# Graph network on one core: the first layer's gathers are released by the landing of the gather two ahead, no longer by TensorE's transposes

## Chip, core and metric

The kernel runs on one core of one Trainium2 chip. The metric is the device time of the whole program in microseconds (us), the median of several runs. TensorE is PE in the profile, VectorE is DVE, ScalarE is ACT, GpSimd is POOL, and SyncE, which only issues DMAs here, is SP.

## What is computed

Two message-passing layers on a graph of 12,500 nodes with 16 features and 412,500 edges sorted by destination. The change touches the first layer alone. Cut to what matters:

```python
h    = relu(edge_attr @ W1 + b1)                # 412500 x 256
w    = (h @ W2 + b2).reshape(-1, 16, 16)        # one 16 x 16 matrix per edge
msgs = einsum('ei,eio->eo', x[src], w)          # x[src]: the gather
aggr = segment_sum(msgs, dst)                   # per node
```

A normalisation of the nodes stands before it, a batch normalisation behind it, and the second layer repeats gather, product and sum with 8 edge features.

## The kernel before

`layer0` cuts the edges into G = 404 groups of 1,024: 8 tiles (T) of 128 edges. For each group, five engines run a loop of their own over the groups, written out by hand, and meet at semaphores (the dictionary `q`). `each_ring` runs a body four groups at a time, so that buffer numbers are constants: the first lap is written out, then a hardware loop, then the last lap.

- SP loads the edge features `ea` of a group (64 KB).
- POOL gathers: `gather(g, r, use)`, lines 795 to 805. For each of the 8 tiles one indirect DMA (L802) fetches 128 rows of 32 floats from `gather_rows` in DRAM into `xg[r]`, one of RING = 4 buffers; its landing raises the semaphore `xg_in[r][t]` by 16. Every fourth group (r = 3, from the second lap on) has only 7 gathers, because PE forms the last tile's rows from a table instead (L947). Ahead of the 8 gathers of a group stands one instruction that waits: for the indices (`idx_ready`, by ACT), for the buffer (`msg_ready` of the group four back, by DVE), and for `e_turned` of group g, which PE raises behind its 8 transposes of that group's edge features. Nothing that the gather reads or writes depends on those transposes. That instruction also adds one to `gathers_begun`, a counter on which nobody waits.
- ACT splits the edge features, copies the transposes out (L835), applies the relu (L841), makes the indices (L816) and splits the messages.
- PE, for each group g: the first product `hidden` (L905), the second product `edge_weights` (L919, two halves of 16 matmuls in float32), the transposes `turn(g + 2)` (L895, they raise `e_turned`), and `scatter(g - 1)` (L933, 16 small matmuls that sum messages into a window of nodes).
- DVE multiplies the edge matrices with the gathered rows in 4 units of 2 tiles (L1002), each of which waits for PE's `wmm` and for the two landings `xg_in`, reduces them (L1009), adds the bias (L1015, raises `msg_ready`), and makes the one-hot tables for the scatter (L1033).

PE transposes for group g + 2 while it works on group g, so a burst of 8 gathers starts about two groups ahead of its use. The second layer (`layer1`) has four scatters for each group on POOL (L1745), each with its own counting instruction ahead of it.

Of the kernel before, what the change touches and what calls it, by code (L numbers as in the profile page):

```python
# [51 lines left out]
def need(engine, sem, count):  # L52

    if isinstance(count, int) and count <= 0:
        return
    engine.wait_ge(sem, count)  # L56
# [15 lines left out]
def each_ring(engine, count, body, ring=4, laps=1):  # L72


    for c in range(laps * ring):
        body(c, c % ring, c // ring)
    assert count % ring == 0
    with engine.Fori(0, count // ring - laps - 1) as i:
        for u in range(ring):
            body(i * ring + (laps * ring + u), u, i + laps)  # L80
    for u in range(ring):
        c = count - ring + u
        body(c, u, c // ring)
# [626 lines left out]
def layer0(nc, S, k, sem, c, ea16, n_passes):  # L710
# [42 lines left out]
    q = {n: sem(n) for n in names}  # L753
    ea_in = [sem(f"ea_in{s}") for s in range(2)]
    xg_in = [[sem(f"xg_in{r}{t}") for t in range(T)] for r in range(RING)]
# [5 lines left out]
    def dense(r, lap):  # L761

        return r in DENSE and not (isinstance(lap, int) and lap == 0)
# [6 lines left out]
    with nc.Fori(0, n_passes) as _:  # L770
        with nc.Block() as block:

            @block.sync
            def _(sp):
                def load(g, r, lap):
                    s = r % 2
                    e0 = min(g * GE, S.E - GE) if isinstance(g, int) else sp.snap(g * GE)
                    need(sp, q["ea_used"], g - 1)
                    sp.dma_start(ea[s][:, :, :].rearrange("p t f -> p (t f)"),
                                 ea16[bass.ds(e0, GE), :].rearrange("(p t) f -> p (t f)", t=T)  # L780
                                 ).then_inc(ea_in[s], 16)
                    if dense(r, lap):
                        need(sp, q["col_free"], lap - 1)
                        sp.dma_start(col_b[:, :], k.col_rows[bass.ds(g, 1), :].broadcast_to([KP, P])
                                     ).then_inc(q["col_in"], 16)
                    if isinstance(g, int) and g == 1:
                        sp.dma_start(rows_in[:, :, :],
                                     k.rows[0:S.N, :].rearrange("(k p r) f -> p k (r f)", p=KP, r=KR)
                                     ).then_inc(q["node_in"], 16)
                each_ring(sp, G, load, RING, 2)  # L790
                clear_tables(sp, S, k, q["zeroed"])

            @block.gpsimd
            def _(pool):
                def gather(g, r, use):
                    pool.wait_ge(q["idx_ready"], g + 1)
                    need(pool, q["msg_ready"], g - RING + 1)
                    if not (isinstance(g, int) and g < 2):
                        pool.wait_ge(q["e_turned"], g + 1)
                    pool.sem_inc(q["gathers_begun"], 1)  # L800
                    for t in range(T - 1 if dense(r, use) else T):
                        pool.indirect_dma_start(  # L802
                            xg[r][:, t, :], None, k.rows,
                            bass.IndirectOffsetOnAxis(ap=idx[r][:, t:t + 1], axis=0)
                        ).then_inc(xg_in[r][t], 16)
                each_ring(pool, G, gather, RING)

                pool.wait_ge(q["msg_ready"], G)
                pool.dma_reset()
# [1206 lines left out]
```

## Time and profile before

| what | value |
|---|---|
| runs shown | 8242.69 us median of 3 (8239.94 to 8244.3) |
| profiled execution, span from the first to the last instruction | 8221.3 us |
| PE, PEld, DVE, ACT, POOL busy | 89%, 78%, 81%, 54%, 69% |
| mean granted TensorE clock | 0.947 of full speed |
| L802, the gathers | 3132, busy 3041.9 us, mean 971 ns; POOL idle before them 1882.4 us |
| L919, the second product | 12928 matmuls, busy 3240.2 us |
| DMA | mean 42 GB/s over the span, about 17 GB/s in the first layer |

For the profiled execution only its span is given; it is 21.4 us below the median of the runs, and what lies around the span is taken as that. Busy means that an engine was executing; an engine can be idle because it waits for another or because its instruction has not reached it. In a timeline row the bracket holds the idle time before the row and what ended it. "issue" there means that no wait ended that the profile shows, and "remote" that the releaser was not an instruction of this list.

### The profile page before, as it was taken

To read this page: it belongs to the slowest core of one execution; us is meant where nothing else is said; L and a number is where in the kernel's file an instruction comes from. 1 tells how busy PE (TensorE), PEld (TensorE's weight loads), DVE (VectorE), ACT (ScalarE), POOL (GpSimd) and SP (SyncE) were. 2 spreads that over 40 slices of the span, in tenths; PEclk is the share of its full clock that TensorE was granted. 3 is DMA by queue.
4 is the path that set the end of the run, shared out by engine and by line. 5 is a ranking of instruction groups with operands and counts; after the bars stand their busy time and mean duration, and the time that the engine had idled before them with its cause. 6 is when DMAs were issued, how large, how long until landed. Compare 5 with 4: busy or idle time off the path is not lost. (4 is left out here: it accounts for less than half of the span.)

```text
span 8221.3 us, 191064 instructions
## 1 busy us (share of the span) xinstructions
PE 7349.2 (89%) x52997; PEld 6446.6 (78%) x52997; DVE 6691.0 (81%) x17449; ACT 4457.4 (54%) x8279; POOL 5696.0 (69%) x4866
## 2 busy tenths in 40 slices
PE   7888888888888888888888886999999999999998
PEld 5667676666676666666676765999999999999996
DVE  6777777777777777777777777999999999999997
ACT  3333333333333333333333335888888878778884
POOL 6666666666666666666666664888888888888886
PEclk8999999999999999999999998999999999999999
DMA  2000000000000000000000014444444455554443
GB/s 60 18 17 17 17 17 17 17 17 17 17 17 17 17 18 17 17 17 18 17 17 17 17 23 101 73 75 74 74 75 74 74 73 74 72 74 75 73 75 64
DMA packets 713464, 341.73 MB, mean 42 GB/s; under 512 B 422115, under 2 KB 656599, under 8 KB 713427
## 3 DMA queue, kind: packets, MB, share of 16 engines
q1 hardware_dynamic: 379313, 272.94, 13.1%
q0 software_dynamic: 332928, 64.86, 12.9%
q10 hardware_dynamic: 1186, 3.51, 0.1%
q8 instruction: 15, 0.25, 0.0%
q14 instruction: 22, 0.18, 0.0%
HBM read 307.85 MB, written 32.96 MB: 41 GB/s over the span
## 5 line engine op out<-in xcount | busy, mean ns | idle before, releaser
L802 POOL DMA_INDIRECT xg<-gather_rows,idx x3132 | 3041.9, 971 | 1882.4 <-issue 1848.5
L919 PE MATMUL ps_w<-W2s,hT 128*128 128x256 f32 x12928 | 3240.2, 408 | 37.1 <-issue 36.6
L919 PEld LDWEIGHTS ps_w<-W2s,hT 128*128 128x128 f32 x12928 | 2678.5, 207 | 581.6 <-issue 97.0
L1745 POOL DMA_INDIRECT sums<-total,row x1616 | 2551.0, 1579 | 529.1 <-issue 474.4
L1708 PE MATMUL ps_wide<-hot_col,placed 128*128 128x392 f32 x12928 | 2434.7, 345 | 4.8 <-DVE placed L1544 2.1
L1708 PEld LDWEIGHTS ps_wide<-hot_col,placed 128*128 128x128 f32 x12928 | 2313.6, 196 | 12.2 <-issue 6.9
L841 ACT ACTIVATE hT<-ps_h,b1c 128x512 f32<-128x512 f32 x1616 | 1022.8, 680 | 2302.1 <-PE ps_h L905 2090.8
L1002 DVE TENSOR_TENSOR prod<-ps_w,xg 128x512 f32<-128x512 f32 x1616 | 1098.1, 690 | 969.7 <-remote 599.7
L1544 DVE SCALAR_TENSOR_TENSOR placed<-ps_r,src_r,halves 128x512 fp32r<-128x512 f32 x1616 | 1097.5, 741 | 0.1
L1643 ACT ACTIVATE square<-iota_col,minus_col 128x784 bf16<-128x784 int16 x1212 | 1061.3, 938 | 66.6 <-issue 58.0
L1009 DVE TENSOR_REDUCE msg<-prod 128x32 f32<-128x512 f32 x1616 | 1058.9, 676 | 0.0
L1649 ACT ACTIVATE hot_col<-square,ones 128x2352 fp32r<-128x2352 bf16 x404 | 910.4, 2253 | 0.0
L933 PE MATMUL ps_a<-parts,hot 128*128 128x48 bf16 x6464 | 347.5, 184 | 549.8 <-issue 534.0
L1033 DVE TENSOR_SCALAR hot<-iota,rel_t 128x256 bf16<-128x256 bf16 x3232 | 729.1, 303 | 116.0 <-DVE ea_res L982 73.0
L933 PEld LDWEIGHTS ps_a<-parts,hot 128*128 128x128 bf16 x6464 | 249.8, 96 | 580.4 <-issue 566.4
L905 PE MATMUL ps_h<-eT,W1p 96*128 96x512 bf16 x1616 | 526.5, 401 | 147.5 <-issue 137.8
L1682 PE MATMUL ps_q<-q_win,hotT 128*128 128x128 bf16 x9696 | 609.6, 219 | 18.9 <-DVE hotT L1483 18.9
L1501 DVE TENSOR_TENSOR prod<-ps_q,e 128x512 f32<-128x512 f32 x808 | 552.3, 684 | 42.6 <-issue 40.4
L1682 PEld LDWEIGHTS ps_q<-q_win,hotT 128*128 128x128 bf16 x9696 | 548.1, 98 | 20.0 <-DVE hotT L1483 20.0
L1510 DVE TENSOR_REDUCE pre<-prod 128x64 f32<-128x512 f32 x808 | 548.3, 679 | 0.1
L851 ACT ACTIVATE parts<-msg_res 128x128 bf16<-128x128 f32 x404 | 124.9, 309 | 552.9 <-DVE msg_res L1021 322.9
L835 ACT ACTIVATE eT<-ps_e 96x1024 bf16<-96x1024 bf16 x404 | 409.1, 1013 | 1.9 <-PE ps_e L895 1.9
(229 smaller groups left out, 5425.0 us busy)
## 6 DMA issues: line engine op xcount, KB each, us to landing
dst_row<-dst_rows SPq DMA_DIRECT2D x404, 256.0 KB
src_row<-src_rows SPq DMA_DIRECT2D x404, 128.0 KB
xg<-gather_rows,idx POOLq DMA_INDIRECT x3132
q_win<-q_rows SPq DMA_DIRECT2D x404, 96.0 KB
ea<-in_edge_attr SPq DMA_DIRECT2D x404, 64.0 KB
sums<-total,row POOLq DMA_INDIRECT x1616
e<-in_edge_attr SPq DMA_DIRECT2D x404, 32.0 KB
q_rows<-Q SPq DMA_DIRECT2D x12, 768.0 KB, 5.4
```

The lines of the kernel that those rows point to most:

```text
L802: pool.indirect_dma_start(xg[r][:, t, :], None, k.rows, bass.IndirectOffsetOnAxis(ap=idx[r][:, t:t + 1], axis=0)).then_inc(xg_in[r][t], 16)
L841: a.activation(hT[s][:, j, :], ps_h[j][:, :], ACT.Relu, bias=k.b1[:, j:j + 1]).then_inc(q["relued"], 1)
L919: last = pe.matmul(to, hT[half][:, j, col:col + P], k.W2[:, j, :], start=(j == 0), stop=(j == 1 and not with_b2))
L1002: v.tensor_tensor(prod[u % 2][:, :, :, :], ps_w[u][:, :, :, :], xg[r][:, 2 * u:2 * u + 2, 0:D].unsqueeze(2).broadcast_to([P, 2, D, D]), AL ...
L1009: v.tensor_reduce(msg[s][:, 2 * u:2 * u + 2, :], prod[u % 2][:, :, :, :], X, ALU.add).then_inc(q["reduced0"], 1)
L1033: last = v.tensor_scalar(hot[s][:, t, :], k.iota[:, :], k.rel[:, bass.ds(g, 1), t:t + 1].rearrange("p g t -> p (g t)"), None, ALU.is_equal)
L1544: last = v.scalar_tensor_tensor(placed[s][:, w, :, :, :].rearrange("p r f a -> p r (f a)"), ps_r[:, :, :], src_r[:, bass.ds(g, 1), w], hal ...
L1643: last = a.activation(square[:, n, :], iota_col[:, :], ACT.Square, bias=minus_col[:, bass.ds(g, 1), WIDE - ACT_TILES + n])
L1649: a.activation(hot_col[s][:, WIDE - ACT_TILES:, :, :].rearrange("p w a b -> p (w a b)"), square[:, :, :].rearrange("p w b -> p (w b)"), AC ...
L1682: last = pe.matmul(ps_q[u][:, w, :, :].rearrange("p h j -> p (h j)"), hotT[s][:, t * P:(t + 1) * P], q_win[s][:, part * P:(part + 1) * P], ...
L1708: last = pe.matmul(ps_wide[:, 2 * r + a, 0:S.LC], placed[s][:, w, r * HR:(r + 1) * HR, :, part].rearrange("p r f -> p (r f)"), hot_col[s][ ...
L1745: pool.indirect_dma_start(k.sums[t], bass.IndirectOffsetOnAxis(ap=row[r][:, t:t + 1], axis=0), total[r][:, t, :], None, compute_op=ALU.add ...
```

## The change

Two edits in `gather`. The wait for `e_turned` goes. From the third tile of a group on (t >= 2), each gather has in front of it an instruction that waits until gather t - 2 of the same group has landed (its semaphore at 16 for each use of the buffer) and adds one to `gathers_begun`. So the first two gathers of a group wait for indices and buffer alone.

```diff
                 def gather(g, r, use):
                     pool.wait_ge(q["idx_ready"], g + 1)
                     need(pool, q["msg_ready"], g - RING + 1)
-                    if not (isinstance(g, int) and g < 2):
-                        pool.wait_ge(q["e_turned"], g + 1)
                     pool.sem_inc(q["gathers_begun"], 1)
                     for t in range(T - 1 if dense(r, use) else T):
+                        if t >= 2:
+                            pool.wait_ge(xg_in[r][t - 2], 16 * (use + 1))
+                            pool.sem_inc(q["gathers_begun"], 1)
                         pool.indirect_dma_start(
                             xg[r][:, t, :], None, k.rows,
                             bass.IndirectOffsetOnAxis(ap=idx[r][:, t:t + 1], axis=0)
```

No instruction of PE, DVE, ACT or SP moves. On POOL, in the hardware loop of the first layer, the first two groups of a lap stood like this before (a row with x7 is seven gathers in a row; the waits are those in front of the row):

```order
L56 REGISTER_ALU [waits idx_ready]
L802 DMA xg<-gather_rows,idx 128x32 [waits msg_ready,e_turned]
L802 DMA xg<-gather_rows,idx 128x32 x7
L796 REGISTER_ALU
L56 REGISTER_ALU [waits idx_ready]
L802 DMA xg<-gather_rows,idx 128x32 [waits msg_ready,e_turned]
L802 DMA xg<-gather_rows,idx 128x32 x7
```

and stand now like this (the second group of the lap; xg_in1t is the landing of tile t in buffer 1):

```order
L56 REGISTER_ALU [waits idx_ready]
L803 DMA xg<-gather_rows,idx 128x32 [waits msg_ready]
L803 DMA xg<-gather_rows,idx 128x32
L803 DMA xg<-gather_rows,idx 128x32 [waits xg_in10]
L803 DMA xg<-gather_rows,idx 128x32 [waits xg_in11]
L803 DMA xg<-gather_rows,idx 128x32 [waits xg_in12]
L803 DMA xg<-gather_rows,idx 128x32 [waits xg_in13]
L803 DMA xg<-gather_rows,idx 128x32 [waits xg_in14]
L803 DMA xg<-gather_rows,idx 128x32 [waits xg_in15]
```

The wait for PE's transposes is gone from the head of the burst, and six waits on landings stand inside it (five in a group of 7 gathers). The gathers themselves keep their order and their number.

## Rows read from the trace of the kernel before

**Rows 1.** Busy time by stretch; 62 to 4960 us is the first layer
```profile
core 0: us, PE busy (x) PEld busy (x) DVE busy (x) ACT busy (x) POOL busy (x), PEclk, DMA share, GB/s
...
500.00:4500.00 4000.00, 3406.92 (x20511) 2782.20 (x20510) 2907.68 (x8081) 1572.46 (x3299) 2479.31 (x2557) 0.92 0.10 17
...
4960.00:8221.00 3261.00, 3152.24 (x27836) 3026.12 (x27834) 3093.25 (x7509) 2507.20 (x4189) 2627.17 (x1696) 0.98 0.50 75
```
**Rows 2.** Groups by line, 500 to 4500 us (busy us, mean ns, idle before)
```profile
L919 PE MATMUL ps_w<-W2s,hT 128*128 128x256 f32 x10558 | 2641.5, 407 | 28.3 <-issue 27.8 <-DVE prod L1002 0.3
L802 POOL DMA_INDIRECT xg<-gather_rows,idx x2557 | 2480.0, 970 | 1523.2 <-issue 1522.6 <-ACT idx L816 0.6
...
L1002 DVE TENSOR_TENSOR prod<-ps_w,xg 128x512 f32<-128x512 f32 x1319 | 895.9, 690 | 801.5 <-remote 509.6 <-issue 165.1 <-PE ps_w L919 43.6
...
L933 PE MATMUL ps_a<-parts,hot 128*128 128x48 bf16 x5264 | 286.1, 184 | 453.8 <-issue 450.0
```
**Rows 3.** Timeline of POOL, three bursts (start us, duration us)
```profile
2510.22 0.95 POOL L802 DMA_INDIRECT xg<-gather_rows,idx  x1 [0.30 <-issue]
2513.62 0.94 POOL L802 DMA_INDIRECT xg<-gather_rows,idx  x1 [2.45 <-issue]
2514.87 0.94 POOL L802 DMA_INDIRECT xg<-gather_rows,idx  x1 [0.30 <-issue]
...
2522.72 0.94 POOL L802 DMA_INDIRECT xg<-gather_rows,idx  x1 [0.30 <-issue]
2526.03 0.94 POOL L802 DMA_INDIRECT xg<-gather_rows,idx  x1 [2.37 <-issue]
...
2537.02 0.94 POOL L802 DMA_INDIRECT xg<-gather_rows,idx  x1 [2.57 <-issue]
```
**Rows 4.** Timeline of PE, 2500 to 2526 us
```profile
2501.09 5.30 PE L919 MATMUL ps_w<-W2s,hT 128*128 128x256 f32 x16
2506.23 0.60 PE L905 MATMUL ps_h<-eT,W1p 96*128 96x512 bf16 x2
2506.67 3.62 PE L919 MATMUL ps_w<-W2s,hT 128*128 128x256 f32 x16
2510.12 0.61 PE L895 MATMUL ps_e<-identb,ea_parts 128*96 128x128 bf16 x8
2510.57 0.44 PE L933 MATMUL ps_a<-parts,hot 128*128 128x48 bf16 x11
2511.18 0.19 PE L933 MATMUL ps_a<-parts,hot 128*128 128x48 bf16 x1 [0.18 <-issue]
2512.60 0.27 PE L933 MATMUL ps_a<-parts,hot 128*128 128x48 bf16 x4 [1.23 <-issue]
```
**Rows 5.** Timeline of DVE, the multiply that waits in each burst
```profile
2512.68 0.69 DVE L1002 TENSOR_TENSOR prod<-ps_w,xg 128x512 f32<-128x512 f32 x1 [1.51 <-remote]
...
2525.20 0.69 DVE L1002 TENSOR_TENSOR prod<-ps_w,xg 128x512 f32<-128x512 f32 x1 [1.65 <-remote]
```
**Rows 6.** POOL's waiting instruction L800, window 2504 to 2505 us
```profile
L800 POOLq EVENT_SEMAPHORE  x1: 8643/8643/8643, 2504.2 to 2504.2; - x1
```
**Rows 7.** DMA traffic, 2510 to 2514 us, 40 slices of 0.1 us
```profile
DMA  0000005610000000004530000000000000000000
GB/s 0 0 0 0 0 0 82 72 10 0 0 0 0 0 0 0 0 0 61 62 41 0 0 0 0 0 0 0 0 0 0 0 0 0 0 0 0 0 0 0
```
**Rows 8.** Timeline, the layer's first burst of 16 gathers
```profile
68.26 1.09 PE L895 MATMUL ps_e<-identb,ea_parts 128*96 128x128 bf16 x8 [0.48 <-DVE ea_parts L989]
68.60 0.95 POOL L802 DMA_INDIRECT xg<-gather_rows,idx  x1 [0.30 <-issue]
69.03 0.26 PEld L905 LDWEIGHTS ps_h<-eT,W1p 96*128 96x128 bf16 x2
69.14 1.06 PE L905 MATMUL ps_h<-eT,W1p 96*128 96x512 bf16 x2
69.38 1.02 ACT L835 ACTIVATE eT<-ps_e 96x1024 bf16<-96x1024 bf16 x1 [0.35 <-PE ps_e L895]
```
**Rows 9.** Groups by line, second layer, 5000 to 8000 us
```profile
L1745 POOL DMA_INDIRECT sums<-total,row x1549 | 2446.2, 1579 | 507.4 <-issue 454.1 <-ACT row L1635 37.1 <-DMA sums<-total,row 16.2
L1708 PE MATMUL ps_wide<-hot_col,placed 128*128 128x392 f32 x12416 | 2336.5, 345 | 4.8 <-DVE placed L1544 2.1 <-issue 0.8
```

## Prediction

> **What bounds the kernel now.** I read the busy time by stretch first. The second layer, from 4960 us on, is not touched; PE and DVE are busy there for 3152 and 3093 of 3261 us. The first layer is looser: in 4000 us PE is busy for 3407, DVE for 2908, POOL for 2479 [rows 1]. The group count of that stretch is that of the second product's matmuls over the 32 of a group, 10558 / 32 = 329.9 [rows 2]. So one group takes 4000 / 329.9 = 12.12 us, and in it PE is busy for 10.33 us, DVE for 8.81 us and POOL for 7.52 us. No engine is full, so a wait that comes back in each group sets the pace.
>
> The groups by line show where. POOL idles 1522.6 us before its gathers, DVE 509.6 us before the multiply, released by something "remote", and PE 450 us before the scatter matmuls with nothing named [rows 2]. The timelines say how these hang together. POOL starts a gather every 1.25 us (0.94 us of work and 0.30 us between two); a burst of eight begins at 2513.62 us, its last gather at 2522.72 us, and the next burst only at 2526.03 us [rows 3]. Between them are 2.4 us of idle POOL. PE ends its transposes at about 2510.7 us (start 2510.12, eight of them) and then hardly moves: one scatter matmul at 2511.18 us, the next at 2512.60 us [rows 4]. At 2512.68 us DVE's multiply is let go, after 1.51 us of idleness; the product it waits for ended on PE 2.4 us before, at 2506.67 + 3.62 = 2510.29 us. The next such release is at 2525.20 us [rows 5]. Both lie 2.46 and 2.48 us behind the start of the burst's last gather, at 2510.22 and 2522.72 us [rows 3, 5]. POOL's waiting instruction is busy from 2504.2 us for 8.64 us, so to 2512.9 us, although the transposes it waits for were done at 2510.7 us [rows 6].
>
> I read it so: while POOL stands in its long wait with gathers still queued behind each other, signals of the other engines come late, and they come through once the last gather has landed. POOL waits for a signal that its own gathers hold back. Two rows speak for this. In the layer's first burst PE ends its transposes at 68.26 + 1.09 = 69.35 us, in the middle of sixteen gathers at the same spacing, and ACT starts on them at 69.38 us, at once; POOL had no wait for PE there [rows 8]. In the second layer POOL issues a DMA of 1.58 us after another, at 4 to 5 times the traffic, and PE loses 4.8 us in 3000 [rows 1, 9]. Why the signals are held, no row tells.
>
> **The change, part by part.** *The wait for the transposes goes.* With it goes the tail between the last gather's start and the next burst, 2526.03 - 2522.72 = 3.31 us, of which 1.25 us would be there in any case. What holds POOL next is the buffer (the message of the group four back), and that is far: POOL is two groups ahead now and may be three ahead.
>
> *A wait on a landing is added before the gathers 2 to 7 of a group.* Its price is the landing time L of a gather from its start, and the time D from the end of a wait to the start of the gather behind it. D is 2513.62 - 2512.9 = 0.73 us [rows 3, 6]. L is not shown and is bounded from both sides: the gather of 2510.22 us has its data packets until 2512.1 us, so L is at least 1.9 us [rows 7]; everything that waited was released 2.47 us after the last start, so L is at most that [rows 3, 5]. I take 2.2 us, midway, since the rise of the semaphore follows the last data packet and the release of the others follows that rise. Then gather t starts L + D = 2.93 us after gather t - 2, where it now starts 2.50 us after it. The two chains, of the even and of the odd tiles, run beside each other, 1.25 us apart. A group of eight lasts 3 x 2.93 for the tiles 2, 4 and 6, and 2 x 1.25 to the next group's first gather, which has no landing to wait for: 11.29 us. A group of seven lasts 10.04 us. The mean over a lap of 3 and 1 is 10.98 us. The gathers last 0.97 us on the mean and not 0.94 [rows 2, 3]; for 7.75 of them that adds 0.2 us: **11.18 us a group**.
>
> The Trainium skill (DMA: Bandwidth & Descriptors, "Anatomy of one DMA — SWDGE (gpsimd) path") puts such a DMA at about 2.0 us and bytes / 436,000, which for the 16 KB of a gather is 2.04 us. By it the step would be 2.77 us, the group 10.70 us, and the whole 574 us shorter than now, about 7668 us. The packets end 1.9 us after the start [rows 7], so the trace does not speak against it, but no row shows the landing itself.
>
> *The counting instructions and register steps* (six more on POOL in a group of eight) are issued while the engine works on the gather before; the gap of 0.30 us stays the same in the second layer, where each DMA has such an instruction. If that cover failed, it would cost at most D again, which is already in the sum. DVE, queued for the landings, gets them later by up to 11.3 - 10 = 1.3 us within a burst, but the burst starts two to three groups ahead of use.
>
> *Who is the bound then.* PE needs at most its 10.33 us. In that are matmuls at the lower clock: the granted clock is 0.92 on the mean in this stretch [rows 1], and the sixteen matmuls right after PE's halt took 5.30 us where the next ones took 3.62 us [rows 4]. DVE needs 8.81 us. Both are under 11.18 us: POOL becomes the bound.
>
> *Sum.* (12.12 - 11.18) x 404 groups = 380 us. The profiled execution's span of 8221.3 us becomes 7841 us; with the 21.4 us by which the median lies above the span, **7862 us**. Ends: with L = 1.9 us the group is 10.28 us, PE's 10.33 us takes over, -723 us, 7520 us. With L = 2.47 us it is 11.99 us, -53 us, 8190 us.
>
> **Rivals.**
> 1. *The signals stay late, and the spread-out burst makes it worse* (the other side). POOL now stands in a wait of about half to one us before nearly every gather, with another gather in flight, and the burst is never quiet. If any waiting of POOL beside gathers holds back signals, as the long one does, PE and DVE get free only behind the last landing of a burst, and the bursts are longer. For: PE's halt, from 2511.2 to 2512.6 us, falls beside the last gather of a burst, while POOL stands in its wait [rows 3, 4, 6]. Against: rows 8, and the short waits end often. Price: last gather at 3 x 2.93 + 1.25 + 0.2 = 10.24 us, and the present tail of 3.31 us: 13.55 us, 12.3 us for seven, 13.24 us on the mean; +1.12 x 404 = +452 us, 8695 us. It decides as soon as more than 0.94 us a group of the halt is left on top of POOL's 11.18 us.
> 2. *The halts are PE's own.* PE's scatter stops for a reason that has nothing to do with POOL's wait, POOL's idle time was harmless, and PE's 10.33 us and its 1.8 us of idleness stay: 12.12 us a group, no change, 8243 us. Against it: DVE's release comes 2.46 and 2.48 us behind the last gather's start in two bursts in a row [rows 3, 5], which fits POOL's clock and not PE's.
> 3. *Half of it.* The long hold goes, a short delay for each signal stays, and PE with its dependences needs about 11.65 us: -190 us, 8053 us. This lies inside the forecast's own bounds.
> 4. *The waits never bite.* That would need L + D under 2.5 us, and 1.9 + 0.73 is 2.63 us. Then the group would fall to PE's 10.33 us, 7520 us. I give it 2 in 100.
>
> **How the numbers follow.** The forecast with POOL as the bound has 0.58, half of it (3) 0.05, no bite (4) 0.02, no change (2) 0.05, slower (1) 0.30. This measurement tells about 0.2%, 16 us, from no change. So faster 0.65, same 0.05, slower 0.30. The forecast's own range is 7520 to 8190 us. The range for 8 in 10 leaves out its lowest tail, under 7600 us (0.04), and the half of rival 1 that lies above 8560 us (0.15): 7600 to 8560 us.
>
> **What would show it.** Right: POOL's timeline alternates between 1.25 and about 1.7 us from start to start, with no gap of 2.4 us at the end of a burst; the group takes about 11.2 us; DVE's idle time before the multiply names the landings or shrinks; PE's scatter matmuls run without single steps; the granted clock of the stretch rises or stays. The landing time can then be read as the step of two gathers less 0.73 us. Wrong: PE's single steps beside gathers are as many as before, or spread over the whole group (rival 1 if the group is above 12.12 us, rival 2 if POOL is seen waiting on the buffer at an unchanged pace). The size is wrong if the step of two gathers is not near 2.93 us.

## The result, and the profile after

| kernel | median | runs | profiled execution, span |
|---|---|---|---|
| before | 8243.49 us | 8239.94 to 8244.47 | 8221.3 us |
| changed | 8299.38 us | 8278.49 to 8306.21 (4 runs) | 8294.4 us, clock 0.949 |

The ratio is 1.0064, with a 95% interval of 1.0052 to 1.0075: the change made the kernel slower by 0.6%, where the prediction had it faster by 4.6%. The time lies inside the range, 7600 to 8560 us, and on the side that had 0.30. Line numbers behind `gather` grow by one: L803 is the gather, L842 the relu, L920 the second product.

Busy time of the changed kernel in the stretch of [rows 1]:

```profile
core 0: us, PE busy (x) PEld busy (x) DVE busy (x) ACT busy (x) POOL busy (x), PEclk, DMA share, GB/s
500.00:4500.00 4000.00, 3356.24 (x20304) 2671.17 (x20303) 2874.96 (x7991) 1544.30 (x3263) 2416.86 (x2528) 0.93 0.10 17
```

The groups by line in that stretch (busy us, mean ns of one, idle before and what ended it), to be read against [rows 2]:

```profile
L920 PE MATMUL ps_w<-W2s,hT 128*128 128x256 f32 x10438 | 2619.7, 406 | 44.4 <-issue 29.1 <-DVE prod L1003 11.3
L803 POOL DMA_INDIRECT xg<-gather_rows,idx x2528 | 2417.4, 956 | 1583.4 <-issue 1014.7 <-DMA xg<-gather_rows,idx 484.2 <-ACT idx L817 83.6
...
L1003 DVE TENSOR_TENSOR prod<-ps_w,xg 128x512 f32<-128x512 f32 x1304 | 873.3, 689 | 236.7 <-issue 53.2 <-remote 43.3 <-DVE hot_c L1044 22.4
...
L842 ACT ACTIVATE hT<-ps_h,b1c 128x512 f32<-128x512 f32 x1306 | 827.9, 680 | 1883.7 <-remote 1384.6 <-PE ps_h L906 393.6 <-issue 101.7
...
L906 PE MATMUL ps_h<-eT,W1p 96*128 96x512 bf16 x1304 | 423.9, 407 | 540.1 <-ACT eT L836 394.7 <-issue 142.6 <-ACT hT L842 0.8
...
L934 PE MATMUL ps_a<-parts,hot 128*128 128x48 bf16 x5216 | 198.6, 183 | 42.0 <-issue 37.7 <-DVE win_sum L1094 1.5
...
L983 DVE TENSOR_TENSOR ea_res<-ea,ea_parts 128x128 f32<-128x128 f32 x326 | 95.0, 291 | 709.9 <-ACT ea_parts L823 432.7 <-issue 276.9
```

A group now takes 4000 / (10438 / 32) = 12.26 us, 0.14 us more than before; over 404 groups that is 57 us, the whole difference of the medians (56 us). The old waits went, as forecast: PE's idle time before the scatter fell from 453.8 to 42.0 us, DVE's before the multiply from 801.5 to 236.7 us, and the "remote" share of the latter from 509.6 to 43.3 us. Others took their place. The first product on PE (L906) waits 540.1 us where it waited 108.6 us before, and DVE waits 709.9 us where it waited 108.0 us to work on the edge features that ACT splits (L983), so its gain before the multiply is used up elsewhere. And the relu on ACT, which before was released by PE, is now let go by "remote" for 1384.6 us. The kernel before, same stretch:

```profile
L841 ACT ACTIVATE hT<-ps_h,b1c 128x512 f32<-128x512 f32 x1319 | 835.2, 680 | 1886.1 <-PE ps_h L905 1748.9 <-remote 79.7 <-issue 41.8
...
L905 PE MATMUL ps_h<-eT,W1p 96*128 96x512 bf16 x1318 | 429.7, 401 | 108.6 <-issue 105.3 <-ACT hT L841 1.6 <-ACT eT L835 1.5
...
L982 DVE TENSOR_TENSOR ea_res<-ea,ea_parts 128x128 f32<-128x128 f32 x330 | 95.4, 289 | 108.0 <-issue 79.8 <-ACT ea_parts L822 27.1
```

POOL, PE and ACT of the changed kernel in time (start us, duration us), to be read against [rows 3, 4]:

```profile
2513.57 0.94 POOL L803 DMA_INDIRECT xg<-gather_rows,idx  x1 [0.30 <-issue]
2515.49 0.94 POOL L803 DMA_INDIRECT xg<-gather_rows,idx  x1 [0.98 <-issue]
2516.74 0.94 POOL L803 DMA_INDIRECT xg<-gather_rows,idx  x1 [0.30 <-issue]
2518.64 0.94 POOL L803 DMA_INDIRECT xg<-gather_rows,idx  x1 [0.96 <-DMA xg<-gather_rows,idx]
```
```profile
2514.53 0.56 PE L934 MATMUL ps_a<-parts,hot 128*128 128x48 bf16 x16
2514.94 0.59 PE L906 MATMUL ps_h<-eT,W1p 96*128 96x512 bf16 x2
2515.37 3.62 PE L920 MATMUL ps_w<-W2s,hT 128*128 128x256 f32 x16
2522.32 1.03 PE L906 MATMUL ps_h<-eT,W1p 96*128 96x512 bf16 x2 [3.33 <-issue]
```
```profile
2520.01 1.26 ACT L842 ACTIVATE hT<-ps_h,b1c 128x512 f32<-128x512 f32 x2 [7.40 <-remote]
```

POOL's pauses of 2.4 us between bursts are gone; it alternates between steps of 1.25 us and about 1.9 us, 3.15 us for two (2515.49 to 2518.64). PE's scatter runs its sixteen matmuls without a stop. But the product `ps_h` that the relu at 2520.01 us needs ended on PE at 2514.94 + 0.59 = 2515.53 us. Measured from there, the signal came 4.5 us late (the profile models the ends of matmuls, so this is a lag behind a modelled end), ACT could not copy the transposes out behind it, and PE's next first product started after 3.33 us of idleness. The late signals did not go away. They moved, from one that the scatter and the multiply wait for to one that the relu waits for.

All of them are signals of PE. In the first layer of every run below with late signals, "remote" stands only in front of work that waits for PE: the relu, the multiply and, in the kernel before, POOL's gathers. The trace's records of semaphores say the same. In the kernel before, from 500 to 3500 us, 246 of the 247 recorded signals of the transposes come more than 0.5 us behind the last transpose, at most 6.1 us; of ACT's and DVE's recorded signals none lags its instruction.

### The profile page after: what moved, and what is told of

Same layout as the page of the kernel before. It is cut to its first block and busy times, and to the rows that moved or that the text cites. A ratio compares the mean times of both kernels' runs of the same rounds, so it can differ in the third digit from the quotient of the medians.

```text
span 8294.4 us, 193483 instructions
## 1 busy us (share of the span) xinstructions
PE 7333.8 (88%) x52997; PEld 6345.0 (76%) x52997; DVE 6680.6 (81%) x17449; ACT 4443.1 (54%) x8279; POOL 5653.6 (68%) x4866
## 5 line engine op out<-in xcount | busy, mean ns | idle before, releaser
L803 POOL DMA_INDIRECT xg<-gather_rows,idx x3132 | 3001.6, 958 | 1996.5 <-issue 1259.3
L920 PE MATMUL ps_w<-W2s,hT 128*128 128x256 f32 x12928 | 3244.2, 406 | 63.0 <-issue 33.9
L920 PEld LDWEIGHTS ps_w<-W2s,hT 128*128 128x128 f32 x12928 | 2632.5, 205 | 627.7 <-issue 126.7
L842 ACT ACTIVATE hT<-ps_h,b1c 128x512 f32<-128x512 f32 x1616 | 1024.7, 680 | 2288.5 <-remote 1662.2
L906 PE MATMUL ps_h<-eT,W1p 96*128 96x512 bf16 x1616 | 526.8, 407 | 656.3 <-ACT eT L836 480.1
L983 DVE TENSOR_TENSOR ea_res<-ea,ea_parts 128x128 f32<-128x128 f32 x404 | 117.7, 291 | 858.3 <-ACT ea_parts L823 512.2
L906 PEld LDWEIGHTS ps_h<-eT,W1p 96*128 96x128 bf16 x1616 | 137.0, 97 | 811.5 <-issue 769.9
```

Source lines behind the costliest of these rows:

```text
L803: pool.indirect_dma_start(xg[r][:, t, :], None, k.rows, bass.IndirectOffsetOnAxis(ap=idx[r][:, t:t + 1], axis=0)).then_inc(xg_in[r][t], 16)
L842: a.activation(hT[s][:, j, :], ps_h[j][:, :], ACT.Relu, bias=k.b1[:, j:j + 1]).then_inc(q["relued"], 1)
L920: last = pe.matmul(to, hT[half][:, j, col:col + P], k.W2[:, j, :], start=(j == 0), stop=(j == 1 and not with_b2))
```

## The experiments

Each session sent one to four kernels to one chip, and the kernel before ran beside them there. The sessions fall into two sorts: the kernel before takes 7298 us in some and 8173 us or more in others, and stays within 0.2% inside each.

| session, number of the chip | before in it | this kernel | ratio (95%) |
|---|---|---|---|
| the result | 8243.49 | changed 8299.38 | 1.0064 (1.0052 to 1.0075) |
| e1 to e4, 7 | 7298.18 | below | |
| e5, e6, 5 | 7298.32 | changed 8126.28 | 1.1136 (1.1118 to 1.1155) |
| e7 to e9, 0 | 8175.45 | below | |
| e10 to e12, 4 | 7298.71 | below | |
| e13, e14, 2 | 8174.14 | below | |
| e15, e16, 6 | 8173.44 | changed 8150.99 | 0.9973 (0.9961 to 0.9985) |
| e17, 6 | 7298.69 | below | |
| e18, 1 | 7298.13 | below | |

I call the two sorts sessions with holds and sessions without; a hold is such a late signal of PE. The session of the result has holds too. The expectations written on the way call them chips with and without holds; that was premature, since two sessions that name chip 6 fell on either side.

### e1 to e4: the parts of the change one by one, and no gathers

**e1** takes the wait for the transposes away and adds nothing:

```diff
-                    if not (isinstance(g, int) and g < 2):
-                        pool.wait_ge(q["e_turned"], g + 1)
```

> The wait for PE's transposes is gone, no wait on landings is added. Theory A (a gather in flight holds back the other engines' signals, whatever POOL itself waits for): a burst now starts as soon as its buffer is free and is no longer placed so that its tail falls on PE's scatter; the holds stay as many and fall on the relu handshake. 8300 to 8600 us, PE's idle time before L905 as in the changed kernel or more. Theory B (POOL's waiting instruction holds them back): POOL waits only for the buffer, 3 groups ahead; 7700 to 8100 us.

Measured: 7300.17 us, ratio 1.0001 (0.9992 to 1.0011).

**e2** keeps that wait and adds the waits on landings:

```diff
                     for t in range(T - 1 if dense(r, use) else T):
+                        if t >= 2:
+                            pool.wait_ge(xg_in[r][t - 2], 16 * (use + 1))
+                            pool.sem_inc(q["gathers_begun"], 1)
```

> The landing waits are added, the wait for PE's transposes stays. Theory A: the burst of eight lasts 3 x 3.13 + 1.25 = 10.6 us to the start of its last gather instead of 9.1, and the pause behind it stays: a group of 12.1 + 1.5 = 13.6 us, 8243 + 600 = about 8850 us. Theory B: the same or a little less, 8600 to 8850 us. A third reading (the holds come only from gathers 1.25 us apart): the holds vanish, a group is about 12.1 us, 8243 us.

Measured: 8129.4 us, ratio 1.1138 (1.1119 to 1.1156).

**e3** adds the counting alone:

```diff
+                        if t >= 2:
+                            pool.sem_inc(q["gathers_begun"], 1)
```

> Only the counting instruction is put in front of each gather from the third on, without a wait. It costs nothing on a queue that runs ahead of its engine: theories A and B both say 8243 us within 16 us. If pacing of POOL's queue by such an instruction is what frees the signals (as in the second layer), it is faster, below 8200 us.

Measured: 7299.32 us, ratio 1.0001 (0.9992 to 1.0011).

**e4** gathers for the first four groups only (DVE's waits on the landings go with the gathers, in a part of the edit that is not shown):

```diff
+                    if not (isinstance(g, int) and g < RING):
+                        return
                     for t in range(T - 1 if dense(r, use) else T):
```

> Left out: all gathers of the first layer from the fifth group on (the rows of the first four groups are used again), with DVE's waits on them. Theories A and B: the holds go with them and PE is the bound at 10.3 us a group or less, 8243 - 1.8 x 404 = 7520 us or less. Rival (PE's halts are its own): no change, 8243 us.

Measured: 7235.3 us, ratio 0.9912 (0.9895 to 0.9929).

None of the delays of the first profile appear on this chip, and the four tell what the parts cost by themselves. Counting: nothing. The wait for the transposes: nothing. All gathers together: 63 us. The waits on landings: 831 us. e1 did not test my theory, as there was nothing held to set free; the times expected for e1 to e3 had assumed holds and were missed, and e4's, 7520 us or less, fits a layer without holds in any case.

### e5 and e6: both kernels again, to see this other regime

The kernels of the change and of before, without an edit.

> The changed kernel as it is, on the chip of this job, against the kernel before in the same job. Where the kernel before takes 7298 us (no holds, PE is the bound at 9.8 us a group), the landing waits make POOL the bound at 11.3 to 11.8 us a group, as with both waits: 7900 to 8130 us, 8 to 11% slower. Where the kernel before takes 8243 us (signals held), 8299 us again.

> The kernel before, for its profile on this chip. Without holds: PE's scatter without single steps, no idle time of DVE before the multiply released by something remote, granted clock 1.00 in the first layer, POOL's pauses at the end of a burst under 1 us. With holds: as in the profile of before.

Measured: changed 8126.28 us against 7298.32 us, ratio 1.1136 (1.1118 to 1.1155); e6, one run, 7304.75 us. The kernel before without holds, 500 to 3500 us (its first layer ends earlier):

```profile
core 0: us, PE busy (x) PEld busy (x) DVE busy (x) ACT busy (x) POOL busy (x), PEclk, DMA share, GB/s
500.00:3500.00 3000.00, 2883.93 (x18937) 2314.94 (x18938) 2653.91 (x7455) 1453.99 (x3041) 2258.30 (x2359) 1.00 0.12 21
```
```profile
L802 POOL DMA_INDIRECT xg<-gather_rows,idx x2359 | 2258.5, 957 | 741.8 <-issue 732.0 <-ACT idx L816 7.3 <-DVE msg L1015 2.4
L919 PE MATMUL ps_w<-W2s,hT 128*128 128x256 f32 x9728 | 2222.8, 381 | 31.7 <-DVE prod L1002 31.7
...
L1002 DVE TENSOR_TENSOR prod<-ps_w,xg 128x512 f32<-128x512 f32 x1217 | 812.8, 689 | 176.6 <-issue 45.7 <-DVE hot_c L1043 33.2
```

PE is busy for 96% of the time at full clock, a group takes 3000 / (9728 / 32) = 9.87 us, nothing is released by "remote", and POOL issues gather after gather at 1.25 us. And the changed kernel there (e5), 500 to 4500 us:

```profile
L920 PE MATMUL ps_w<-W2s,hT 128*128 128x256 f32 x10795 | 2578.8, 392 | 64.9 <-DVE prod L1003 64.1
L803 POOL DMA_INDIRECT xg<-gather_rows,idx x2612 | 2479.3, 949 | 1522.7 <-DMA xg<-gather_rows,idx 933.5 <-issue 578.9 <-ACT idx L817 10.3
...
L1003 DVE TENSOR_TENSOR prod<-ps_w,xg 128x512 f32<-128x512 f32 x1348 | 900.7, 688 | 869.9 <-DMA xg<-gather_rows,idx 683.9 <-PE ps_w L920 64.0 <-issue 48.1
L842 ACT ACTIVATE hT<-ps_h,b1c 128x512 f32<-128x512 f32 x1348 | 848.5, 680 | 694.9 <-PE ps_h L906 691.2 <-issue 3.3
```

A group takes 4000 / (10795 / 32) = 11.86 us. POOL waits for landings and DVE for POOL's gathers: POOL is the bound, cleanly, as the prediction had it, only at a higher price. (11.86 - 9.87) x 404 = 804 us, against 828 us measured. The page of this kernel also gives the landing time that the prediction had to bound (the last number, us from issue to landing; the page of the changed kernel in the first result has the same line, and so has e8's, in a session with holds):

```profile
xg<-gather_rows,idx POOLq DMA_INDIRECT x3132, 2.4
```

With L = 2.40 us and D = 0.73 us [rows 3, 6] the step of two gathers is 3.13 us; POOL's timeline in e5 has 3.20 us and 3.09 us for two such steps:

```profile
2506.43 0.94 POOL L803 DMA_INDIRECT xg<-gather_rows,idx  x1 [0.95 <-DMA xg<-gather_rows,idx]
...
2509.63 0.94 POOL L803 DMA_INDIRECT xg<-gather_rows,idx  x1 [1.00 <-DMA xg<-gather_rows,idx]
...
2512.72 0.95 POOL L803 DMA_INDIRECT xg<-gather_rows,idx  x1 [0.90 <-DMA xg<-gather_rows,idx]
```

### e7 to e9: what holds the signals

All three met a session with holds. **e7** is the changed kernel with `t >= 3` and `t - 3` in place of 2, so the waits allow three gathers in flight.

```diff
-                        if t >= 2:
-                            pool.wait_ge(xg_in[r][t - 2], 16 * (use + 1))
+                        if t >= 3:
+                            pool.wait_ge(xg_in[r][t - 3], 16 * (use + 1))
```

> No wait for the transposes; from the fourth gather on each waits for the landing of the gather three ahead. Theory C (on a chip without holds the whole cost of the change is POOL's chain: landing 2.40 us + 0.73 us from the wait's end to the next start = 3.13 us a step): a step of three gathers lasts 3.75 us anyway, the wait ends at 2.40 us, 0.62 us ahead of need; no cost, 7298 us within 16 us. Theory D (waiting instructions inside the burst cost by themselves, whatever they wait for): between 7298 and 8126 us, in the middle. If the chip of this job holds signals (kernel before at 8243 us), theory A says about 8250 us or more.

Measured: 9092.6 us, ratio 1.112 (1.1102 to 1.1139).

**e8** is the changed kernel with `t >= 1` and `t - 1`: a gather waits for the one right ahead of it. Only the first gather of a group still starts 1.25 us behind the last one of the group before.

```diff
-                        if t >= 2:
-                            pool.wait_ge(xg_in[r][t - 2], 16 * (use + 1))
+                        if t >= 1:
+                            pool.wait_ge(xg_in[r][t - 1], 16 * (use + 1))
```

> Each gather from the second on waits for the landing of the one in front of it. Theory C: 3.13 us from gather to gather, 7 x 3.13 + 1.25 = 23.2 us for a group of eight, 20.0 us for seven, 22.4 us on the mean; 7298 + (22.4 - 9.8) x 404 = about 12390 us, and 3.13 us can be read from POOL's timeline. Any other step contradicts the sum of the two.

Measured: 12498.75 us (one run).

**e9** is the kernel before with one more load of 400 KB in each group, issued by SP:

```diff
+                    if not (isinstance(g, int) and g < 2 * RING):
+                        sp.wait_ge(q["node_ready"], 1)
+                        need(sp, q["hog"], 16 * (g - 2 * RING))
+                        sp.dma_start(rows_in[:, 0, :], k.rows[0:KP * KR, :].rearrange("(p r) f -> p (r f)", r=KR)
+                                     ).then_inc(q["hog"], 16)
```

> The kernel before with one more load of 400 KB for each group of the first layer on SP's queue (data that nobody reads), some 40 GB/s more than the 21 GB/s there are. Theory E (the holds of the first profile are a matter of DMA traffic of any kind beside the gathers): PE's single steps and late releases appear, 7600 to 8300 us. Rival (the traffic has nothing to do with them): 7298 us within 60 us.

Measured: 8185.7 us, ratio 1.0012 (1.0002 to 1.0023), at 51 GB/s in place of 17.

The relu's row of e8, 500 to 4500 us:

```profile
L842 ACT ACTIVATE hT<-ps_h,b1c 128x512 f32<-128x512 f32 x704 | 442.6, 679 | 367.0 <-PE ps_h L906 366.8
```

And two gathers of e8 where two groups meet:

```profile
2502.25 0.94 POOL L803 DMA_INDIRECT xg<-gather_rows,idx  x1 [2.12 <-DMA xg<-gather_rows,idx]
2503.49 0.94 POOL L803 DMA_INDIRECT xg<-gather_rows,idx  x1 [0.30 <-issue]
```

e8 is the telling one. It is slow, because every gather but the first of a group waits out a landing (4000 / (5649 / 32) = 22.66 us a group, where 22.4 us were expected), but "remote" has gone from the relu altogether, although POOL stands in more and longer waits than anywhere else: it is idle for 2708 of 4000 us. So POOL's waiting does not hold signals; a run of gathers that overlap does. With one in flight, and two for about 1.15 us of each group (2502.25 + 2.40 - 2503.49), nothing is held. e7 allows three, but with 1.25 us from start to start and a landing after 2.40 us the third starts when the first is in, so two is the most; there the relu waits 2101.9 us for "remote", and 1384.6 us in the changed kernel (another session), whose two overlap for less of the time. Three times the bytes moved by SP's loads change next to nothing (e9), so it is not traffic of that kind; no expectation for e9 had covered a session with holds.

Overlap alone is not enough either. In the kernel before, a burst began at 2501.16 us, and in the middle of it the relu starts 0.42 us behind the start of its product:

```profile
2506.23 0.60 PE L905 MATMUL ps_h<-eT,W1p 96*128 96x512 bf16 x2
...
2506.65 1.26 ACT L841 ACTIVATE hT<-ps_h,b1c 128x512 f32<-128x512 f32 x2 [0.58 <-issue]
```

In the bursts that began at 2501.16 and 2513.62 us, and in e13's of 2499.63 us below, the last signal of PE that passes at once is recorded 5.7, 7.2 and 5.8 us behind the burst's first gather; the later ones are held until about the last landing. What decides it, no run shows.

### e10 to e12: three parts in one session

e10 is e1's kernel, e11 is e2's. **e12** moves the copies to SP and makes them plain: fixed rows of the same table in the same size, not the edges' own, and POOL has nothing to do in the layer:

```diff
+                    need(sp, q["msg_ready"], g - RING + 1)
+                    for t in range(T - 1 if dense(r, lap) else T):
+                        sp.dma_start(xg[r][:, t, :], k.rows[P * t:P * (t + 1), :]
+                                     ).then_inc(xg_in[r][t], 16)
...
-                        pool.indirect_dma_start(
-                            xg[r][:, t, :], None, k.rows,
```

> Again the wait for the transposes alone taken away. On a chip where the kernel before takes about 8200 us (signals held, as on the chips of the first result and of the run with lag three): theory F (overlapping gathers hold signals; the old wait keeps the end of each burst, where all is released, next to PE's scatter, and so protects the relu handshake): about 9090 us, as with lag three, whose waits hardly bite. If instead the waits of lag three cost there, it is nearer to 8200 us. On a chip where the kernel before takes 7298 us: 7300 us again.

> Again the landing waits with the wait for the transposes kept. On a chip that holds signals, theory F: the last gather of a burst starts at 3 x 3.13 + 1.25 = 10.6 us instead of 9.1 us and the pause of 3.3 us stays, if signals are held to the end of the burst: 13.6 us a group, about 8800 us. If two gathers that overlap only in part let signals through, POOL's chain of 11.8 us a group is the bound: 8130 to 8300 us. On a chip without holds 8129 us again.

> Changed: the rows of the first layer are fetched by plain copies of the same size (128 rows of 128 bytes, fixed rows) that SP issues, 8 or 7 a group, in place of POOL's indirect gathers. On a chip that holds signals: if POOL's own DMAs (their descriptors written by POOL) are the cause, the holds go and the time is near 7300 us; if any overlapping DMAs of 128 short rows do it, it stays near 8200 us or above. On a chip without holds: 7240 to 7300 us.

Measured: e10 7298.85 us, ratio 0.9999 (0.999 to 1.0009); e11 8128.52 us, 1.1138 (1.112 to 1.1157); e12 7293.69 us, 0.9994 (0.9984 to 1.0004). The session had no holds. It repeats e1 and e2 and settles nothing about the holds.

### e13 and e14: the two parts in a session with holds

The kernels of e1 and e2 again.

> The wait for the transposes alone taken away, hoped for on a chip that holds signals (kernel before at about 8200 us). Theory F (the old wait keeps the release at the end of each burst next to PE's scatter): about 9090 us, as with lag three. Rival (the waits of lag three made its cost): nearer to 8200 us. On a chip without holds 7300 us, which tells nothing new.

> The landing waits with the wait for the transposes kept, hoped for on a chip that holds signals. Theory F with signals held to the end of a burst: 13.6 us a group, about 8800 us. If signals come through at the seams between two gathers that overlap only in part: POOL's chain of 11.8 us is the bound, 8130 to 8300 us.

Measured: e13 9123.77 us, ratio 1.1158 (1.1125 to 1.119); e14 8161.43 us, ratio 0.9985 (0.9973 to 0.9996). This is the experiment that e1 should have been, and it contradicts the prediction head on: taking away the wait that I held to be the culprit costs 950 us (the expectation for it, made after e7, was near: 9090 us). The rows of e13, 500 to 4500 us (two lines fewer in `gather`, so L800 is the gather, L839 the relu, L917 the second product):

```profile
500.00:4500.00 4000.00, 3170.39 (x17346) 2373.44 (x17345) 2476.73 (x6826) 1300.53 (x2784) 2044.34 (x2158) 0.88 0.08 15
```
```profile
L917 PE MATMUL ps_w<-W2s,hT 128*128 128x256 f32 x8906 | 2548.5, 428 | 544.7 <-issue 530.8 <-DVE prod L1000 5.7
L800 POOL DMA_INDIRECT xg<-gather_rows,idx x2158 | 2044.6, 947 | 1956.0 <-ACT idx L814 1347.9 <-issue 608.1
...
L839 ACT ACTIVATE hT<-ps_h,b1c 128x512 f32<-128x512 f32 x1114 | 700.6, 679 | 2255.3 <-remote 2235.9 <-PE ps_h L903 17.8 <-issue 1.3
```

And its timelines, POOL, then ACT, then PE:

```profile
2499.63 0.94 POOL L800 DMA_INDIRECT xg<-gather_rows,idx  x1 [5.01 <-ACT idx L814]
...
2508.36 0.94 POOL L800 DMA_INDIRECT xg<-gather_rows,idx  x1 [0.31 <-issue]
2514.26 0.94 POOL L800 DMA_INDIRECT xg<-gather_rows,idx  x1 [4.96 <-ACT idx L814]
```
```profile
2511.14 1.26 ACT L839 ACTIVATE hT<-ps_h,b1c 128x512 f32<-128x512 f32 x2 [8.34 <-remote]
2513.20 0.21 ACT L814 ACTIVATE idx<-src_t 128x8 int32 x1
```
```profile
2509.55 0.47 PE L917 MATMUL ps_w<-W2s,hT 128*128 128x256 f32 x1 [0.34 <-issue]
2510.26 0.38 PE L917 MATMUL ps_w<-W2s,hT 128*128 128x256 f32 x1 [0.24 <-issue]
```

Here the loop can be read off. A burst runs from 2499.63 us, its last gather starts at 2508.36 us. The relu comes 2.78 us behind that start, so 0.38 us behind a landing of 2.40 us: its signal is held to the end of the burst. ACT makes the indices for the next burst only behind that relu, at 2513.20 us, and the burst starts at 2514.26 us. The sum is 8.73 + 2.78 + 2.06 + 1.06 = 14.63 us; the mean group is 4000 / (8906 / 32) = 14.37 us (every fourth burst has one gather less). So a burst holds the very signal on which the next one depends, and the two take turns. PE itself stutters in the same stretch: its second product runs in single matmuls with pauses between (L917 idles 530.8 us by "issue", where e6 has 31.7 us, all of it a wait for DVE), though within such a run of eight matmuls no wait stands in the program. So it is not only that others hear of PE late; "held signal" names what the waiting engine sees. e7 does the same (14.31 us a group): a wait for the gather three back hardly bites, since three steps of 1.25 us are 3.75 us and L + D is 3.13 us.

### e15 and e16: plain copies and the change, in a session with holds

e15 is e12's kernel, with the same fixed rows; e16 is the changed one.

> Plain copies of fixed rows, issued by SP, in place of POOL's gathers (same sizes, 8 or 7 a group), hoped for on a chip that holds signals. If POOL's own DMAs (descriptors written by POOL) are the cause of the holds: about 7300 us, as on the chip without holds. If any overlapping DMAs of 128 short rows hold signals: 8200 us or more. On a chip without holds 7294 us again.

> The changed kernel once more, hoped for on a chip that holds signals, in the same job as the kernel before. There the landing waits alone gave 8161 us and the missing wait for the transposes is now free to put the holds on the relu handshake: above 8174 us by about the 0.6% of the first result, 8200 to 8240 us. On a chip without holds 8126 us again.

Measured: e15 7303.43 us, ratio 0.8937 (0.8911 to 0.8963); e16 8150.99 us, ratio 0.9973 (0.9961 to 0.9985). With the copies on SP the layer runs at its pace without holds, in a session where the kernel before takes 8173 us. Its rows, 500 to 3500 us, and then SP's copies of one group in its timeline:

```profile
500.00:3500.00 3000.00, 2886.88 (x18979) 2319.21 (x18978) 2653.08 (x7466) 1457.45 (x3048) 0.00 (x0) 1.00 0.11 21
```
```profile
L833 ACT ACTIVATE hT<-ps_h,b1c 128x512 f32<-128x512 f32 x1220 | 767.1, 679 | 514.7 <-PE ps_h L897 514.4
```
```profile
2505.21 3.64 SPq L792 DMA_DIRECT2D xg<-gather_rows  x8
```

Each transfer has the size it had, a group has as many, they wait for no transposes and for no landings, they overlap more densely (eight issued within 3.64 us, each landing 1.7 us later), and nothing is "remote". The 870 us that such a session adds to the kernel before belong to POOL's overlapping gathers.

And e16, 500 to 4500 us:

```profile
L920 PE MATMUL ps_w<-W2s,hT 128*128 128x256 f32 x10753 | 2578.8, 394 | 19.9 <-DVE prod L1003 11.8 <-issue 4.9
...
L842 ACT ACTIVATE hT<-ps_h,b1c 128x512 f32<-128x512 f32 x1344 | 853.1, 681 | 1495.3 <-remote 967.2 <-PE ps_h L906 446.2 <-issue 79.8
```

The same kernel as in the first result, at 11.90 us a group: there are holds still, 967.2 us before the relu, but they add only 0.04 us to POOL's own 11.86 us. The expectation of 8200 to 8240 us, which took the first result's 0.6% for a property of such sessions, was missed.

### e17 and e18: plain copies issued by POOL

What e15 leaves open is whether it takes POOL as the issuer, the indirect addressing or the scattered rows. These keep POOL and its waits, without the one for the transposes, and copy fixed rows:

```diff
-                        pool.indirect_dma_start(
-                            xg[r][:, t, :], None, k.rows,
-                            bass.IndirectOffsetOnAxis(ap=idx[r][:, t:t + 1], axis=0)
-                        ).then_inc(xg_in[r][t], 16)
+                        pool.dma_start(xg[r][:, t, :], k.rows[P * t:P * (t + 1), :]
+                                       ).then_inc(xg_in[r][t], 16)
```

> The e_turned wait removed, and the gathers replaced by plain copies of the same size (128 rows of 128 bytes, fixed rows, not the edges' own), still issued by POOL with the same waits for indices and buffer. On a chip where the kernel before takes about 7298 us every theory expects about 7300 us. On a chip where it takes about 8174 us: if any overlapping DMAs issued by POOL hold back signals, holds as in the kernel without the e_turned wait (9124 us there), at least over 7600 us, with ACT's relu released by 'remote'; if it takes the indirect addressing, 7300 us as with the copies on SP.

> The kernel of e17 again, which had a chip without holds (before 7298.69 us there). If this chip shows holds (before about 8174 us): plain overlapping copies by POOL hold back signals if it comes above 7600 us; it takes the indirect addressing if it comes at about 7300 us.

Measured: 7290.35 us, ratio 0.9989 (0.9979 to 0.9998), and 7293.48 us, ratio 0.9994 (0.9985 to 1.0004). Both sessions had no holds, so neither decides it.

## Why the prediction was wrong

In sessions with holds the two edits give these times:

| | no waits on landings | waits on landings |
|---|---|---|
| wait for transposes | 8174 (before; 8243 in the result's session) | 8161 (e14) |
| no wait for transposes | 9124 (e13) | 8151 (e16; 8299 in the result's session) |

And without holds: 7298 (before) and 8129 (e2) in the upper row, 7300 (e1) and 8126 (e5) in the lower. The waits on landings put the kernel on POOL's chain, 8126 to 8161 us in e2, e5, e14 and e16, each in a session of its own; that happens to be about as long as the kernel before is with its holds, and the change trades one for the other.

**The step that failed first: "POOL waits for a signal that its own gathers hold back", so that without this wait the holds go.** The first half stands, for PE's signals: they come through behind a burst's last landing [rows 5, 6], and e8, e13 and e15 show it in three ways. The prediction spoke of the signals of the other engines; those of ACT and DVE are never seen late. The second half was wrong. The holds need gathers in flight, not a waiting POOL (e8: POOL waits most, nothing is held), and taking POOL's wait away alone makes them dearer (e13, +950 us). By its rows, the wait for the transposes did useful work by its place: the late part of each burst fell beside scatter and multiply, which cost 2.25 us a group (12.12 - 9.87), while the relu's signal passed early in the burst. Without it, the late part of a burst meets the relu's handshake, from which the first product and the next burst's indices hang, and that costs 4.50 us a group (14.37 - 9.87, each from another session). That it is the place which does it is my reading of the timelines; no run moved the burst by itself. It also shows that the prediction named the wrong next wait: not the buffer of the group four back, but the indices (1347.9 us before the gathers of e13). In the result the holds moved to the relu just so, 1384.6 us before it. I had taken the signal at 69.38 us [rows 8], which came at once beside sixteen gathers, for proof that a POOL without such a wait holds nothing. Two things were wrong with it. Signals pass early in steady bursts too. And POOL did stand in a wait for PE there: its waiting instruction for the third group began at 69.1 us and lasted 18.04 us, in the kernel before:

```profile
L800 POOLq EVENT_SEMAPHORE  x1: 18044/18044/18044, 69.1 to 69.1; - x1
```

In that same burst PE's next recorded signal, of the second product that ended at 74.31 us, stands at 77.65 us in the trace's semaphore records, 3.3 us late. Nor did [rows 9] say what I took from it: the second layer's DMAs also overlap, starting some 1.9 us apart (1.58 and 0.30 us) and landing after 3.0 us (e6's page), and PE loses little there with holds or without; why they do so little, no run shows.

**The term that was mis-sized: L.** I took 2.2 us between the ends 1.9 and 2.47 us; it is 2.40 us. By the prediction's own formula a group of eight then takes 3 x 3.13 + 2 x 1.25 = 11.89 us, one of seven 10.64 us, the mean 11.58 us, with 0.2 us for the longer gathers 11.78 us. Measured without holds: 11.86 us. The form of the sum was right, and its upper end (11.99 us, 8190 us) was the place to be. A release 2.47 us behind the last start [rows 5] was the nearer row: it is a signal that has passed, where the end of the data packets at 1.9 us [rows 7] is only traffic. The Trainium skill (DMA: Bandwidth & Descriptors, "Anatomy of one DMA — SWDGE (gpsimd) path") gives 2.04 us by its figures. The trace has 2.4 us for the indirect gather, so the measurement decides, and the estimate by the page, 7668 us, was further off than mine; POOL's plain copies of the same size landed after 2.0 us (e17), as the page has it.

**The parts together.** The first result lies 8299 - 8126 = 173 us above the same kernel without holds. That rest, 12.26 - 11.86 = 0.40 us a group, or 162 us, is what the remaining holds add on top of POOL's chain. In e16 they add 0.04 us. Why the first result had more of them than e16, the runs don't tell.

**D, 0.73 us, was right.** L + D = 3.13 us, and the steps measured are 3.09 to 3.20 us, which with L = 2.40 us leaves 0.69 to 0.80 us for D.

**The counting at nothing was right** (e3, ratio 1.0001).

**PE's need of 10.33 us was too high.** It holds matmuls at the lower clock behind each halt. Undisturbed, the clock is 1.00 in the stretch and the group 9.87 us (e6). It played no part, as POOL was slower in any case.

**The marks.** No pause of 2.4 us, no single steps in the scatter, DVE's idle time before the multiply less, the clock of the stretch no lower (0.93 after 0.92): these all came, and the time still rose. They were marks of the old holds alone and would not have caught a hold at another handshake. The mark of size did catch it: a step of two of 3.15 us where 2.93 us was said.

**The rivals.** Rival 1, "the signals stay late", is the one that came about, but not as priced. It set the tail of 3.31 us on top of a whole burst, 13.24 us a group and 8695 us; measured are 12.26 us. I read it so, untested: with waits on landings there is a stretch in each step of two, from a landing to the next gather's start, in which one gather alone is in flight, and signals get through near it (the gather of 2516.74 us lands at 2519.14 us, the next starts at 2519.89 us, the relu at 2520.01 us). Its point of decision, more than 0.94 us a group on top of 11.18 us, was passed with 1.08 us, of which some 0.68 us is POOL's own chain (11.86 - 11.18) and 0.40 us holds. Rival 2, PE's own halts, is excluded by e15, where they are gone in a session with holds. Rival 3, half of the gain at 8053 us, lay 246 us too low. Rival 4 is excluded by each POOL timeline.

**What stays open.** What makes a session one with holds: not the kernel, as the same file ran in both, and not simply the chip's number. Whether POOL's plain copies hold signals too (e17, e18). How POOL's gathers can hold PE's signals and not those of ACT and DVE, and whether it is the signal that is late or PE's completion of the matmul, whose end the profile only models. Whether the recording of the profile takes part: in the traces with overlapping gathers and holds, many semaphore records are missing (their pages give no landing time for the gathers, save the first result's), and no run stands beside them that settles it. And the sign of the change where there are holds: 1.0064 in one session, 0.9973 in another, each with an interval clear of 1.

## What to carry to other kernels

A wait on a transfer's landing makes a chain of landing time plus the time from wait to start, here 2.40 + 0.73 us for every two gathers, and is only free while that is shorter than the work of the engine that sets the pace; take the landing from the last release behind it, not from the end of its packets. Before taking away a wait that guards no data, ask where in the other engines' work it puts the burst, and what would meet the burst if it ran on its own clock. If signals seem to come late beside transfers, ask first whose signals they are, then vary the number in flight (a run with one in flight told here) and run the kernel before in several sessions: a difference of 0.6% here stood on a kernel that itself differs by 12% from session to session.

## What the runs showed of the hardware that was not expected

- The same kernel takes 7298 us in five sessions and 8174 to 8243 us in four, steady within 0.2% in each. Of the 870 us between them in e15's session, nearly all is gone when POOL's gathers are replaced by plain copies on SP (e15, 7303 us).
- In sessions with holds, PE's signal to another engine can come more than 4 us late (4.5 us at 2520.01 us) beside gathers of POOL that overlap, while ACT's and DVE's are not late. In e13 ACT starts at 2500.92 us on what DVE ended at 2500.88 us, with two gathers in flight. With one gather in flight there is no such wait (e8), and 51 GB/s of other traffic adds 0.1% (e9).
- An indirect gather of 128 rows of 128 bytes lands 2.4 us after its issue; the plain copy of the same size takes 1.7 us on SP (e15) and 2.0 us on POOL (e17), by the issue rows of their pages:

```profile
xg<-gather_rows SPq DMA_DIRECT2D x3132, 16.0 KB, 1.7
```
```profile
xg<-gather_rows POOLq DMA_DIRECT2D x3132, 16.0 KB, 2.0
```
